# Zeroing the rows behind the expert regions: eight stores of the sync queue, or eight GpSimd scatters

## The reference, cut to what matters

```python
x = x + tanh(g_xattn[0]) * L0_xattn(layernorm(x), ctx, ctx)   # 16 heads, 64 sequences of 64
x = x + tanh(g_ffn[0])   * L0_ffn(layernorm(x))               # 8 experts, top 2, SwiGLU, HID 256
x = x + tanh(g_xattn[1]) * L1_xattn(layernorm(x), ctx)        # similarity attention
x = x + tanh(g_ffn[1])   * L1_ffn(layernorm(x))               # 8 experts, top 2, GELU, rank 64
```

```python
logits = xf @ Wg
top_w, top_i = top_k(logits, 2); top_w = softmax(top_w)
combine = einsum('nk,nke->ne', top_w, one_hot(top_i, 8))
h = einsum('nc,ech->enh', xf, W1); g = einsum('nc,ech->enh', xf, W2)
y = einsum('enh,ehc->enc', silu(h) * g, W3)
out = einsum('enc,ne->nc', y, combine)
```

## Time and profile before

| | us |
|---|---|
| median of 3 runs | 526.86 |
| lowest and highest of these | 526.04, 530.32 |
| time of the profiled execution | 527.54 |
| its span, first to last instruction | 525.6 |

### The profile page before, as it was taken

One profiled execution on the slowest core, in us unless ns is written; L12 is line 12 of the kernel. 1 busy time (PEld: TensorE's weight loads), 2 busy tenths in 40 slices (PEclk: granted clock), 3 DMA queues, 4 the chain that ended last, 5 costly groups with the idle time before them and its releaser, 6 DMA issues. The chain is left out here.

```text
span 525.6 us, 14274 instructions
## 1 busy us (share of the span) xinstructions
PE 478.1 (91%) x4366; PEld 386.0 (73%) x4366; DVE 417.8 (79%) x1684; ACT 308.3 (59%) x750; POOL 224.3 (43%) x312
## 2 busy tenths in 40 slices
PE   2688999898999999989799999998998999899997
PEld 1366777676767777777588788766897878778897
DVE  5788899999999988777557767686699995777973
ACT  1567877777777667545355565557553557453553
POOL 3322155555555454545000066663568773224420
PEclk9999999999999999999889999999999999998999
DMA  9601011000001111125465444321001112000011
GB/s 248 283 11 53 12 40 37 30 31 30 30 30 35 34 50 34 33 72 157 124 179 166 120 125 131 103 77 31 22 21 27 45 47 67 10 2 1 2 41 40
DMA packets 45021, 34.58 MB, mean 66 GB/s; under 512 B 5922, under 2 KB 41122, under 8 KB 44708
## 3 DMA queue, kind: packets, MB, share of 16 engines
q1 hardware_dynamic: 30036, 20.54, 12.9%
q0 software_dynamic: 4128, 8.40, 5.6%
q10 hardware_dynamic: 10800, 4.92, 3.3%
HBM read 21.85 MB, written 11.99 MB: 64 GB/s over the span
## 5 line engine op out<-in xcount | busy, mean ns | idle before, releaser
L1677 PE MATMUL bank<-QK 128*64 128x256 f32 x512 | 70.4, 397 | 9.5 <-ACT QK L611 5.4
L491 POOL DMA_INDIRECT yg<-done,gidx x64 | 64.0, 1000 | 31.5 <-issue 16.0
L475 POOL DMA_INDIRECT sent<-xr,rowu x60 | 58.8, 979 | 35.8 <-DVE rowu L1017 21.7
L457 POOL TENSOR_TENSOR ve<-mv,half 128x4 f32<-128x4 f32 (+1 forms) x40 | 8.3, 208 | 126.2 <-DVE mv L831 125.3
L623 ACT ACTIVATE PT<-bank 128x512 f32<-128x512 f32 x64 | 36.4, 602 | 34.4 <-PE bank L1643 33.7
L1677 PEld LDWEIGHTS bank<-QK 128*64 128x64 f32 x512 | 32.3, 139 | 28.2 <-DVE Pr L914 7.2
L1246 DVE TENSOR_TENSOR act<-sil,bank 128x256 f32<-128x256 f32 x71 | 29.8, 420 | 28.5 <-ACT sil L673 25.5
L673 ACT ACTIVATE sil<-bank 128x256 f32<-128x256 f32 x71 | 27.2, 383 | 37.7 <-PE bank L1834 37.7
L910 DVE TENSOR_REDUCE mx<-bank 128x8 f32<-128x512 f32 x64 | 43.6, 681 | 3.9 <-PE bank L1677 3.7
L1850 PE MATMUL bank<-f0w_s,aT 128*128 x284 | 45.3, 283 | 0.8 <-DVE yb L1252 0.8
L914 DVE TENSOR_TENSOR Pr<-bank,mx 128x512 f32<-128x512 f32 x64 | 43.7, 682 | 1.2
(11 more groups left out here) (246 smaller groups left out, 1295.7 us busy)
## 6 DMA issues: line engine op xcount, KB each, us to landing
xb<-sent SPq DMA_DIRECT2D x71, 64.0 KB, 2.4
done<-yb ACTq DMA_DIRECT2D x71, 64.0 KB
cT<-ctx_t_dram SPq DMA_DIRECT2D x16, 128.0 KB, 2.1
f0w_s<-f_w_dram SPq DMA_DIRECT2D x1, 2048.0 KB, 11.1
Pr<-ctx_t_dram SPq DMA_DIRECT2D x8, 256.0 KB
QK<-ctx_tok_dram SPq DMA_DIRECT2D x8, 256.0 KB
out_dram<-xs SPq DMA_DIRECT2D x8, 256.0 KB, 2.3
xs<-x_dram SPq DMA_DIRECT2D x2, 512.0 KB, 5.7
```

The lines of the kernel that those rows point to most:

```text
L475: nc.gpsimd.indirect_dma_start(sent, bass.IndirectOffsetOnAxis(ap=rowu[:, s, 2 * k + c:2 * k + c + 1], axis=0), rows[:, c, :], None).then_ ...
L491: nc.gpsimd.indirect_dma_start(yg[:, s, j, :], None, done[0:NG1 * P, :] if u < UG else done, bass.IndirectOffsetOnAxis(ap=gidx[:, s, j:j + ...
L1677: last = mm(bank[g % 2][L * b:L * (b + 1), 256 * p:256 * (p + 1)], QT[:, s, g, t:t + L], Kb[:, s, :, t:t + L], start=True, stop=True)
```

## The change

The eight zero stores leave the sync queue. `tail` gets 128 partitions, and VectorE adds the partition's number to each, so that column e holds the 128 rows behind region e. GpSimd issues eight scatters of the zero tile with these row numbers, behind its last scatters of unit 15. Those four lose their waits for transposed blocks. `half_sent(1)` stays as it is.

```diff
-        tail = sb("tail", [1, E], U32)
+        tail = sb("tail", [P, E], U32)
...
-            def zero_after(e):
-
-                if e == 0:
-                    sp.wait_ge(S("tail"), 1)
-                r = sp.value_load(tail[0:1, e:e + 1], min_val=e * REGION, max_val=e * REGION + TOKENS)
-                sp.dma_start(sent[bass.ds(r, P), :], zero[:]).then_inc(S("tails"), 16)
...
-                if 16 <= t < 16 + E // 2:
-                    zero_after(2 * (t - 16))
-                    zero_after(2 * (t - 16) + 1)
...
-            send(UA - 1, 1, (13, 14, 15, 16))
+            def zero_after(first, last):
+
+                for e in range(first, last):
+                    nc.gpsimd.indirect_dma_start(sent, bass.IndirectOffsetOnAxis(ap=tail[:, e:e + 1], axis=0), zero[:], None).then_inc(S("tails"), 16)
+
+            pool.wait_ge(zeroed, 16 * E)
+            send(UA - 1, 1)
+            wait_alone(pool, S("tail"), 1)
+            zero_after(0, E)
...
-                    nc.vector.tensor_copy(tail[:], run[0:1, :]).then_inc(S("tail"), 1)
+                    nc.vector.tensor_scalar(tail[:], run[:], cst[:, C_P:C_P + 1], None, ALU.add).then_inc(S("tail"), 1)
```

## The result

The changed kernel takes 522.16 us (median of 4 runs, 519.03 to 523.40), the kernel before 527.15 us (4 runs). The ratio is 0.9876, with a 95% interval of 0.9831 to 0.9921: 0.8 to 1.7% faster. The forecast of 520.3 us was 1.9 us too low. 522.16 lies in the stated range of 518.8 to 524.2 us, but outside the narrower 519.3 to 521.5 us of the case in which all waits are gone, and it is nearer to the first rival's 523.1 us. So the time alone doesn't say which of the two happened; the profile does. The profiled execution took 523.40 us with a span of 521.5, 4.1 us less than the span before.

A forecast was written before the change was run, and what follows sets the result against it. The sync queue's eight zero stores were taken to bound steps 16 to 21; 0.8 + 3.1 + 2.6 us saved, 6.6 in all, from the median 526.86 gives 520.3 us. The 8-in-10 range was 518.8 to 524.2 us.

The forecast's parts named there:

- the case in which all waits are gone: The main forecast: no step from 16 on waits for its load; 519.3 to 521.5 us, chance 0.70.
- first rival: Scatters take 1.5 us or more apiece, TensorE waits one to two us at step 25; 523.1 us, chance 0.15.
- The queue's four turns: Sync queue from load 16 to load 20: shrinks from 16.45 to about 7.6 us without the eight stores.
- Steps 16 to 21: TensorE's corner in stage b: step 21 starts at 259.9 instead of 266.45, 6.55 us saved.
- step 20: TensorE's step just before step 21, put at 1.5 us; it took 2.77 us before the change.
- The split into a long wait (3.1 us) and 2.6 us of two slow steps: Savings within the corner: 3.1 us in step 18 with its long wait, 2.6 in slow steps 19 and 20.
- The scatters: GpSimd's twelve at 1.25 us each from 244.6, landing 2.3 us after the last start; load 25 out at about 261.5.
- GpSimd against VectorE: Scatters beside VectorE's table work: four more short operations might lose 0.2 us each, 0.8 us of VectorE's time.
- The wait at block 25: Sync queue waits for the scatters before load 25; as a rival, TensorE waits one to two us, chance 0.15.
- The transfers as the cause: Rival: transfers, not their issue, delay the loads; steps 18 to 20 still wait, near 526 us, chance 0.11.
- The slower case: Rival: scatters beside VectorE's work take 3 us or more, load 25 comes late; 533.5 us at worst, chance 0.04.
- the three signs of being wrong: Step 25 waits; loads 17 to 20 land late though issued early; third, step 21's 6.6 us are missing at the end.

The follow-up runs named there:

- b_stores: Kernel before, region-end zeros stored early, turns 16 to 19 storing eight times 64 KB of zeros at fixed rows without reading row numbers: 522.79 us, ratio 0.9920.
- b_fill: Kernel before with 13 matmuls that nobody reads ahead of step 19's wait: 527.61 us, ratio 1.0021.
- b_nozero: Kernel before with the rows behind the regions zeroed at the start, at row numbers known beforehand, and no zeroing in turns 16 to 19: 522.37 us, ratio 0.9919.
- a_double: Changed kernel with sixteen scatters of zeros instead of eight, block 25 waiting for all: 530.94 us, ratio 1.008.
- b_spread: Kernel before with the same eight reads and stores, one in each of turns 17 to 24 instead of two in 16 to 19: 525.94 us, ratio 0.9989.
- a_repeat: Changed kernel once more, unaltered: 522.12 us, ratio 0.9905.
- a_waits: Changed kernel with unit 15's four scatters waiting for transposed blocks again: 522.20 us, ratio 0.9906.
- b_reads: Kernel before, region-end zeros stored early, turns 16 to 19 still reading two row numbers each but storing nothing: 522.27 us, ratio 0.9922.

## Why the prediction was right, and where it was off

**The bound.** Right: the sync queue's own work made the loads late, and not the transfers (`b_stores`: same bytes, no delay). The 1.1 us for a read with its store stand nearly: 0.57 and 0.42 measured apart make 0.99. The queue's four turns were put at 7.6 us and took 7.3 (load 16 at 245.84, load 20 at 253.10).

**Steps 16 to 21.** Forecast 255.1 for step 18 and 259.9 for step 21, from 251.37. Set back by the 0.84 us that this execution was late, they came at 255.20 and 260.51. The corner saved 5.94 us where 6.55 was said. The term that was mis-sized is step 20: put at 1.5 us, it took 261.35 - 259.22 = 2.13. It isn't the chance of one execution: in the nine other profiles with no late load there, step 20 takes 1.99 to 2.18 us. The table wasn't late either (its last row ends at 258.87). In the middle of the step TensorE's queue reads a word of the table into a register (L1810, `load_word`), 0.3 to 0.5 us and some register work, and steps 12 and 20 both have it (step 12 took 2.01 us, in both kernels). That the read is the cause is argued from its place; no run took it out. Its cost isn't fixed: of the later steps that have it, every eighth, step 28 takes 1.47 us, its read done ahead at 272.0, and step 36 takes 1.94. The mean of 1.72 us for steps 12 to 15 in the prediction had such a read in it, and the 1.5 us for step 20 had none. I had thought of the read only as something that might come too early for the table:

```profile
L1810 PEldq TENSOR_LOAD <-table x10: 297/304/492, 219.8 to 341.5; - x10
```

**What the corner consisted of.** Wrong in its working, though not in its sum. The split into a long wait (3.1 us) and 2.6 us of two slow steps reads as if each could be removed by itself. `b_fill` took away the slow clock and gained 0.7 us by step 26, and no time. The sum held because it was made the other way, by walking the steps forward without the late loads; for the split itself the good sum is luck.

**The scatters.** 1.26 us each for 1.25, the first of the four at 245.53 (244.7 when set back, 244.6 was said), landing 3.0 us in the median where 2.3 was taken. That was the wrong row: 2.3 is the median over all scatters, and those of this stretch took 3.3 in the kernel before. Load 25 came at 263.50, 262.7 when set back, 1.2 later than said, of which 0.7 is the landing. It was still in time, so the added wait cost nothing.

**GpSimd against VectorE.** The write of `tail` took 0.22 us, with a scatter beside it that ran on for 0.6 us. The cast of `rowu` again took 0.36 us beside a scatter and ended with it within 0.03 us. The kernel before has sixteen of these casts. Fourteen had no scatter beside them and took 0.17 us; of the two that had one, that at 233.38 took 0.17 and unit 15's 0.37. So the longer time shows only beside a scatter, but not beside every one. The whole cost of twelve scatters in the corner is 0.2 us (`b_nozero`), and eight more made no step longer. The Trainium skill (SBUF — State Buffer, "A bandwidth-pool intuition that's wrong (but worth ruling out)") gives some 3.1 us for a GpSimd DMA held up by a VectorE copy. That showed in none of the runs: in the changed kernel and in `a_double` every scatter of zeros took 0.95 to 0.96 us, with VectorE's operations as short as here. The Trainium skill (DMA: Bandwidth & Descriptors, "Issuing engines are not separate DMA queues") says that starting DMAs on several engines saves only sequencer time, usually small. It is right on what is saved; here that time, 1.1 us eight times, was what the 6 us hung on.

**The rivals.** The wait at block 25 (0.15) wasn't there, but it is near: with the scatters' waits put back, load 25 has 2.2 us instead of 3.8, and step 27 waits 0.49 us. The transfers as the cause (0.11) fell with `b_stores`; they lengthen single loads once the lead is gone (3.85 us in `b_spread`). The slower case (0.04) has its mechanism shown by `a_double`: twice the scatters, and the kernel is slower than the old one.

**What the time lacked.** Of the forecast gain of 6.6 us the corner gave 6.0. The medians of the two sets of runs give 5.0 and 4.7 us, the ratios 6.5 and 5.0. The profiled executions differ by 4.1 us, since the changed one had two more short stretches of low clock. So of the three signs of being wrong that the prediction names, the third came in part: at step 21 5.1 us are gained, and at the end 4.1. One thing stays open: the change removes up to 5.8 us at half clock from an execution, and yet the mean granted clock in `a_repeat` (six executions, 0.992 on average) is hardly above that of the kernel before beside it (nineteen, 0.991). Over the 41 executions of the changed kernel, `a_waits`, `b_nozero`, `b_reads` and `b_stores` it is 0.993, against 0.990 in the 95 of the kernel before; 0.0055 more was to be expected. Part of that may be that not all of the latter had the low clock in full. Whether the other places also fall more often once the corner is gone, and why, wasn't tested.

## What to carry to other kernels

Count what a queue has to issue in each turn, register reads and stores alike, against the time of one turn of the engine that it feeds: 1.1 us for a read and a store, eight times within four turns, ate a lead of 6.4 us, and dealing the same work out over more turns did not help, while moving it to an engine that stood idle did. When a wait is followed by slow steps, don't price the two apart before asking what would be late next; walk the steps forward without the cause instead. And when the moved work gets a waiter of its own, double it once: that gives the price of the new wait and how much room is left.

## What the runs showed of the hardware that I had not expected

- Short falls of the granted clock (0.3 to 1.5 us lost each, where it could be measured) came at a few fixed places of this program, some of them behind idle gaps of only 0.4 to 0.8 us, in some executions and not in others, with the same instructions and the same gaps: near 359 us a gap of 0.79 us lay ahead in the changed kernel, where the clock fell, and in `a_waits`, where it didn't. Waits of 2.47 to 7.30 us for a block load were followed by the low clock in all five profiles that had one.
- A DMA start on the sync queue, 0.33 us otherwise, sometimes took 1.3 to 2.1 us: load 17 before (2.05) and in `b_stores` (1.90), a 256 KB load in the changed kernel (1.35). It comes near a 256 KB load or a pair of stores, though not always; what decides it stays open.
- The landing of a scatter depends on where it lies: 2.3 us in the median over all of the kernel before, 3.3 us for its four from 245 to 251 us, 3.0 us for those of the zero tile in the same stretch of the changed kernel. A price from a median over the whole program was too low in the stretch that counted.
